# Perceiver block on one core: state sums partly inside the loop, K rotated ahead of the third attention's sum, head groups reordered, clears by ACT, GpSimd's rounding moved

## The reference, cut to what matters

```python
x = x + xattn0(layernorm(x), ctx, ctx)            # 16 heads of 16, 2048 keys
x = x + ssm(layernorm(x), A_log, D, W_xproj)      # 16 states: h = exp(dt*A)*h + dt*B*x; y = C.h + D*x
x = x + lora_moe(layernorm(x))                    # base product + top 2 of 16 rank-16 experts
x = x + xattn1(layernorm(x), ctx, mask)           # one head of 256, 2048 keys, key mask
x = x + attn(layernorm(x))                        # 16 heads of 128: local keys, 8 compressed keys, a sink
x = x + moe(layernorm(x))                         # 8 experts, 256->512->512->256, top 2 by gate
```

## Time and profile before

| | us |
|---|---|
| median of 3 runs (lowest, highest) | 493.5 (490.94, 493.93) |
| the profiled execution | 491.93 |
| its span, first to last instruction | 490.1 |
| TensorE busy | 418.6 (85%) |
| VectorE busy | 334.4 (68%) |
| ACT busy | 267.0 (54%) |
| GpSimd busy | 110.0 (22%) |
| mean granted clock of TensorE | 0.975 |
| share of the chain that ended last: TensorE, VectorE, ACT | 63%, 18%, 7% |

### The profile page before, as it was taken

The page is one execution under the profiler, slowest core; times in us unless marked ns, Lnnn a source line. Parts: engine busy times, 40 slices in busy tenths (PEclk is TensorE's granted clock), DMA queues, the critical chain, the costliest instruction groups (busy, mean ns, idle before and its releaser), DMA issues.

```text
span 490.1 us, 9082 instructions
## 1 busy us (share of the span) xinstructions
PE 418.6 (85%) x3628; PEld 307.4 (63%) x3628; DVE 334.4 (68%) x537; ACT 267.0 (54%) x594; POOL 110.0 (22%) x88
## 2 busy tenths in 40 slices
PE   0168789998978898998998889996999799999997
PEld 0115556665645586486444624445889689999996
DVE  3788766678568977894366654865554788877872
ACT  4405887776758717431233315556771286777762
POOL 3002346001294010000022352233000203333300
PEclk9999999999989999999999979998899799999999
DMA  6599186543751078137200000019300595540000
GB/s 226 130 256 277 25 202 174 141 120 90 185 197 48 3 235 305 44 123 297 95 1 1 0 3 0 1 45 361 109 2 0 168 346 175 172 172 1 1 2 23
DMA packets 25002, 58.28 MB, mean 119 GB/s; under 512 B 5209, under 2 KB 13689, under 8 KB 21114
## 3 DMA queue, kind: packets, MB, share of 16 engines
q1 hardware_dynamic: 24960, 57.69, 37.2%
HBM read 44.77 MB, written 0.29 MB: 92 GB/s over the span
## 4 chain that ended last, share of the span: by engine, by line
PE 63%; DVE 18%; ACT 7%; issue 6%; POOL 2%; DMA 2%; SPq 0%; ACTq 0%; DVEq 0%; POOLq 0%
PE ps L1289 19%; PE ps L1093 9%; PE ps L924 7%; PE ps L911 5%; PE ps L880 4%; DVE mx L1666 3%; ACT reg_b L683 3%; PE ps L959 2%; PE ps L1254 2%; PE ps L1244 2%; PE ps L1243 2%; PE ps L1003 2%; POOL qreg L472 2%; PE ps L1090 1%; DMA x<-in_x 1%
## 5 line engine op out<-in xcount | busy, mean ns | idle before, releaser
L1666 DVE TENSOR_REDUCE mx<-ps 128x1 f32<-128x1024 f32 x64 | 77.0, 1221 | 36.5 <-PE ps L880 24.9
L683 ACT ACTIVATE reg_b<-ps 128x512 f32<-128x512 f32 x128 | 74.9, 598 | 26.6 <-PE ps L911 17.2
L911 PE MATMUL ps<-qreg,reg_b 98*128 98x128 bf16 x512 | 47.3, 225 | 5.7 <-ACT reg_b L683 4.2
L1093 PE MATMUL ps<-reg_b,xT 128*128 128x512 f32 x96 | 49.8, 643 | 0.0
L1289 PE MATMUL ps<-part_a 128*128 128x256 f32 x384 | 48.2, 283 | 0.4 <-DVE part_a L1819 0.4
L911 PEld LDWEIGHTS ps<-qreg,reg_b 98*128 98x128 bf16 x512 | 35.2, 100 | 19.8 <-ACT reg_b L683 9.7
L1289 PEld LDWEIGHTS ps<-part_a 128*128 128x128 f32 x384 | 46.9, 192 | 0.6 <-DVE part_a L1819 0.6
L396 POOL TENSOR_TENSOR rstd<-ve,cf 128x1 f32<-128x1 f32 x12 | 6.8, 567 | 174.0 <-DVE ve L1362 174.0
L822 ACT ACTIVATE reg_a<-ps,b 128x256 f32<-128x256 f32 x64 | 30.2, 472 | 24.4 <-PE ps L1289 24.4
L924 PE MATMUL ps<-reg_b 128*32 128x128 f32 x1024 | 43.0, 285 | 0.3 <-ACT reg_b L683 0.3
L880 PE MATMUL ps<-reg_b,qreg 96*128 96x512 bf16 x96 | 34.3, 427 | 10.2 <-DMA reg_b<-reg_b 7.5
(11 more groups left out here) (279 smaller groups left out, 849.1 us busy)
## 6 DMA issues: line engine op xcount, KB each, us to landing
reg_b<-in_w SPq DMA_DIRECT2D x16, 512.0 KB, 7.6
reg_b<-in_w SPq DMA_DIRECT2D x8, 1024.0 KB, 7.3
reg_b<-reg_b SPq DMA_DIRECT2D x56, 128.0 KB, 3.2
reg_b<-in_w_qkv SPq DMA_DIRECT2D x3, 2048.0 KB, 7.5
reg_b<-reg_a SPq DMA_DIRECT2D x40, 128.0 KB, 3.2
reg_a<-in_ctxK SPq DMA_DIRECT2D x4, 1024.0 KB, 7.5
reg_a<-in_ctx SPq DMA_DIRECT2D x8, 512.0 KB, 4.7
reg_b<-bc_mem SPq DMA_DIRECT2D x4, 1024.0 KB, 6.6
```

What stands on the lines that cost most here:

```text
L683: sc.activation(pT[n % 3], score_b[n % 2], ACT.Exp).then_inc(S("exp_done"), 1)
L911: mm = pe.matmul(cols, kS[g % 3][0:SROWS, c // 8, j, P * (c % 8):P * (c % 8 + 1)], qT[b][0:SROWS, HPG * hg + j, :], start=not last, stop=True)
L1093: mm = pe.matmul(bank(b, n % 2), xT[b][:, i, :], w_qkv[j][:, i, 512 * n:512 * (n + 1)], start=False, stop=i == KD - 1)
L1666: ve.reduce_max(mx[:, piece // 2, piece % 2:piece % 2 + 1], score_a[m % 2].rearrange("p i k -> p (i k)"), X_AXIS).then_inc(S("max_done"), 1)
```

## The change

- `sum_states(0, 0)` goes into the last group of the loop, four states each behind chunks 9, 11, 13 and 15; VectorE's products with C and scans take turns for it.
- Behind the loop: 18 fillers first, `x_to_columns(2, 0)` before `step_sizes(1)`, `lora_products(0)` before `state_maps(1)`; ACT and VectorE follow. The key mask is loaded earlier, to another place, and computed earlier; bias0 counts on another semaphore.
- `square(0, 1)` on ACT ahead of `exp3(1)`; `rotated_to_columns(0, 1)` and its copies behind the third attention's output product of batch 1; `add3(1)` and the normalisation behind the whole of `rope_k(0)` instead of within it.
- `clear_values` on ACT, as a copy scaled by zero.
- Head groups: group 0's transposes and mixing ahead and between the scores of groups 1 and 2; VectorE copies the mixed values of group n-2, not n-1.
- GpSimd rounds expert 0's weights only after six groups' weights are normalised (`pr_norm` 12), and those of expert 1 after `x_split`. VectorE's rests of expert 0 all move into the end of the fourth attention. 24 fillers between the last two transposes of x. GpSimd also waits for `nm_done` 6 within the decay exponents.

```diff
 xmask = view(reg_b, 18432, 2048, BF16)
-mask8 = reg_b[0:1, 12544:12544 + NB * KEYS // 4]
+mask8 = reg_b[0:1, 8192:8192 + NB * KEYS // 4]
 mask_row = xmask[0:1, :]
...
     values_in(NG - 1)
+    load(mask8, io["mask"], "mask_in")
...
     sp.wait_ge(S("hc_done"), KD)
-    load(mask8, io["mask"], "mask_in")
-    load(bias0, io["bias0"].partition_broadcast(P), "mask_in")
+    load(bias0, io["bias0"].partition_broadcast(P), "ssm_in")
     load(ctxT[:, 0, :, :], io["ctxT"][0].rearrange("(h p) k -> p h k", p=P), "ctxT_in0")
...
         for n in range(0, NS, 4):
+            if (h, n) == (0, 12):
+                pool.wait_ge(S("nm_done"), 6)
             pool.tensor_tensor(decay[0][:, h, n:n + 4],
...
-    def clear_values(b):
...
-        pool.wait_ge(S("x_done1"), (4, 3)[b])
-        pool.memset(cvs[b][:, :, :, :], 0.0).then_inc(S("cleared"), 1)
...
     compressed_inv_rms(0)
-    clear_values(1)
     rotated_inv_rms(0, 1)
     inv_sqrt(4, 1)
-    clear_values(0)
+    pool.wait_ge(S("xn_done1"), 5)
     compressed_values(0)
...
     pool.wait_ge(S("expert_in0"), 48)
+    pool.wait_ge(S("pr_norm"), 12)
     round_weights(0, 0, "w13_high")
...
     inv_sqrt(5, 1)
-    for b in range(NB):
-        pool.wait_ge(S(f"x_done{b}"), 5)
+    pool.wait_ge(S("x_split"), NB)
     for e in range(1, NE):
...
+    def clear_values(b):
...
+        if b == 0:
+            sc.wait_ge(S("p3T_ps"), 8)
+        sc.wait_ge(S(f"x_done{b}"), 3)
+        sc.activation(cvs[b].rearrange("p g j d -> p (g j) d"), ident.unsqueeze(1).to_broadcast([P, NH, HD]),
+                      ACT.Copy, scale=0.0).then_inc(S("cleared"), 1)
...
     transposed_x(1, 1)
+    transposed_x(2, 0)
     copy_z(1)
     softplus_exp(1)
-    transposed_x(2, 0)
     hidden_exp(0)
...
     transposed_x(3, 1)
+    clear_values(1)
+    square(0, 1)
     rotated_columns(0, 0)
...
     projected(0, 2, range(0, 1))
-    for i in range(2):
+    for i in range(4):
         p3_columns(1, i)
-    square(0, 1)
-    for i in range(2, 4):
-        p3_columns(1, i)
+    clear_values(0)
     projected(0, 2, range(1, 2))
+    rotated_columns(0, 1)
     transposed_x(4, 1)
...
     block_columns(1)
-    rotated_columns(0, 1)
     key_tail(0)
...
-    for n in range(NB * NHG):
+    weight_columns(0)
+    weights(1)
+    for n in range(1, NB * NHG):
         if n + 1 < NB * NHG:
...
-    def sum_states(b, h):
+    def sum_states(b, h, states=range(NS)):
...
         pe.wait_ge(S("hc_done"), KD * b + h + 1)
-        for n in range(NS):
+        for n in states:
             mm = pe.matmul(bank(b, 0)[:, P * h:P * (h + 1)], state[b][:, h, n, :], ident, start=n == 0, stop=n == NS - 1)
-        if h == KD - 1:
+        if h == KD - 1 and n == NS - 1:
             mm.then_inc(S("y_ps"), 1)
...
               (5, 2): [(keep_busy, 6, 18)],
-              (5, 4): [(misc_read, "o_all", 5), (state_maps, 0)],}
+              (5, 4): [(misc_read, "o_all", 5), (state_maps, 0)]}
+    for i in range(4):
+        beside[7, 9 + 2 * i] = [(sum_states, 0, 0, range(4 * i, 4 * i + 4))]
     read_before_rows = {2: ("qT_sb", 4), 3: ("qT_sb", 6), 5: ("z_sb", 1), 6: ("bc_copied", 1)}
...
-    sum_states(0, 0)
     sum_states(0, 1)
+    keep_busy(7, 18)
     x_to_columns(1, 1)
     keep_busy(7, 4)
+    x_to_columns(2, 0)
     step_sizes(1)
+    lora_products(0)
     state_maps(1)
-    keep_busy(7, 3)
-    x_to_columns(2, 0)
-    keep_busy(7, 6)
-    lora_products(0)
     keep_busy(7, 6)
...
     projection(0, 2, range(1, 2))
+    rotated_to_columns(0, 1)
     x_to_columns(4, 1)
...
     block_entries(1)
-    rotated_to_columns(0, 1)
     projection(1, 1, range(2, 4))
...
     rotated_to_columns(1, 1)
-    pe.wait_ge(S("kT_tail"), 4)
-    pe.wait_ge(S("qkT_sb"), 16)
-    pe.wait_ge(S("proj_sb"), len(PROJECTIONS))
-    scores4(1)
     pe.wait_ge(S("cvs_done"), HPG * NB)
...
-    for n in range(NB * NHG):
+    weights_to_columns(0)
+    pe.wait_ge(S("kT_tail"), 4)
+    pe.wait_ge(S("qkT_sb"), 16)
+    pe.wait_ge(S("proj_sb"), len(PROJECTIONS))
+    scores4(1)
+    scores4(2)
+    mix_values(0)
+    for n in range(1, NB * NHG):
         if n + 2 < NB * NHG:
...
         weights_to_columns(n)
-        if n >= 1:
+        if n >= 2:
             mix_values(n - 1)
...
     for b in range(NB):
+        if b == 1:
+            keep_busy(7, 24)
         pe.wait_ge(S(f"x_done{b}"), 5)
...
     def lora_add(b):
-        ve.wait_ge(S("mask_in"), 32)
+        ve.wait_ge(S("ssm_in"), 48)
         link(ve.tensor_tensor(x[b][:, :], x[b][:, :], bias0, ALU.add))
...
-        ve.wait_ge(S("mask_in"), 32)
+        ve.wait_ge(S("mask_in"), 16)
         ve.tensor_scalar(mask_row[0:1, :], mask8.bitcast(U8), 16.0e30, -16.0e30, ALU.mult, ALU.add)\
...
     scan(0, 0)
+    read_states(0, 0)
     scan(0, 1)
-    read_states(0, 0)
     read_states(0, 1)
+    key_mask()
+    add_inputs(0)
     weigh_outputs(1)
...
     ln_stats(1, 1)
-    add_inputs(0)
-    ln_apply(1, 1)
-    key_mask()
     add_states(0)
     ln_stats(2, 0)
+    ln_apply(1, 1)
     ln_apply(2, 0)
...
     max3(1, 1)
-    rope_k(0, [(add3, 1), (ln_stats, 4, 1), (ln_apply, 4, 1)])
+    rope_k(0, [])
+    add3(1)
+    ln_stats(4, 1)
+    ln_apply(4, 1)
     block_scores(1)
...
             score_max(1)
+        if n >= 2:
+            mixed(n - 2)
         if n + 2 < NB * NHG:
             score_max(n + 2)
-        if n >= 1:
-            mixed(n - 1)
     lower_weights(0, 0)
+    lower_weights(0, 1)
+    mixed(NB * NHG - 2)
+    lower_weights(0, 2)
     for b in range(NB):
...
             .then_inc(S("g_shift"), 1)
-    lower_weights(0, 1)
-    lower_weights(0, 2)
     def gate_weights(b):
```

## The result

The changed kernel takes 479.15 us (median of four runs, 478.81 to 483.96), the kernel before 492.42 (four runs, 490.94 to 493.93): a ratio of 0.975, with a 95% interval of 0.971 to 0.979. The forecast was 481.0. The profiled execution took 479.39 us with a span of 477.6, against 490.1 before: 12.5 less. The median fell by 13.3, and the single executions of the changed kernel spread by 5 us.

A forecast was written before the change was run, and what follows sets the result against it. The kernel was taken as bound by hand-offs, with TensorE's gaps each followed by half clock. 0.4 - 7.6 - 6.3 + 1.8 = -11.7 from 491.93 gave 480.2, by medians 481.8; predicted 481.0, range 477 to 486.

The forecast's parts named there:

- part D: Up to the experts, 380 to 397 us: fillers help hidden1, half clock falls on hidden2; +1.8, from -1.7 to +3.3.
- Part A: State sums moved into the first attention's loop, 164 to 186 us: +0.4 us, from -1.5 to +1.5.
- 0.47 of each 0.89 is covered by ACT and 0.42 is not: In the loop, each insertion of four sums takes 0.89 us, of which ACT's time hides 0.47.
- B is just hidden: Behind the loop, the B matrix lands at 191.6, 2 us later, yet in time for state_input at 191.52 + 0.4.
- Part B: K rotated ahead of the third attention's sum, 262 to 304 us: -7.6 us, from -4 to -8.5.
- The 0.4 put down for hand-offs to ACT: Around K's rotation, 0.4 us taken off the sum of gains 1.2 + 3.84 + 3.0.
- Part C: Head groups, 330 to 363 us: smaller gaps, full clock and a shorter period; -6.3 us, from -2.2 to -7.
- the rivals on the period: Head groups: the period stays at 4.48 and only the gaps are won; 483 us, chance 0.13.
- on K being late: Projections: K is late or another gap holds, and half clock is back; 484.8 us, chance 0.10.
- on the slower loop: Head group loop runs at half clock, 7.8 us a group instead of 4.05; 500 us, chance 0.03.
- on no fall of the clock in D: Before the experts, the clock doesn't fall, as gaps are shorter than the earlier 3.03 us; 479.0 us, chance 0.22.
- the one on B's matrix: Behind the first attention's loop, B's matrix lands late, its load sharing queues with the ctxT load; 482.5 us, chance 0.07.

The follow-up runs named there:

- three: Changed kernel with GpSimd waiting for the seventh maxima, fillers between hidden1(0) and hidden2(0), and state_maps(1) ahead of lora_products(0): 475.14 us, ratio 0.966.
- pool_clear: Changed kernel with the two clears back on GpSimd in their old places, K's rotation still ahead of the third attention's sum: 480.48 us, ratio 0.977.
- casts_early: Changed kernel without GpSimd's wait for six groups' weights, so its three casts of expert 0 start early: 482.93 us, ratio 0.980.
- K late: Changed kernel with K's square, reduction, rotation and transposes back in their old places, clears still on ACT: 485.27 us, ratio 0.986.

## Why the prediction was right, and where its steps were off

The forecast of 481.0 was 1.9 above the median, and each part came within about 1 us in the table. That their errors partly cancel in the sum (-0.8) is luck, and so in part is part D. One slip made no difference: the range took A's bounds as 1.1 either way, while -1.5 lies 1.9 from +0.4.

**Part A, +0.4 forecast, +1.0 measured, and 0.35 brought along.** The order of events was right: states ready in time, y early (1.0 us instead of 1.9), the maps late, LoRA's step behind their copy. The failed step is "0.47 of each 0.89 is covered by ACT and 0.42 is not": an insertion costs 0.57. Four sums take about 1.0 within the loop, where the prediction took the 0.89 of those behind it; the cover of 0.47 was right. So the sums behind the loop start 2.4 later counted from the scan, not 1.7. With y 1.0 early and nothing waiting for it, the whole part is a loss; the runs with it undone show this twice. The prediction's own sign of being wrong, LoRA's first step later than by 1 us, was even met in the timeline (186.21 against 185.03, 1.18 later); counted from the first scan it is 0.83. "B is just hidden" held too, and `three` found its edge: 1.2 us earlier and it isn't.

**Part B, -7.6 forecast, -8.35 measured.** Each step came within 1.2 us: exp3(1) 1.5 earlier (1.53), K's reduction at 266.85 (265.65), rotation ready 276.9 (276.0), x normalised 280.0 (279.1), no gap, full clock. About 0.9 of each delay is what had come in ahead of this part, 1.35 instead of 0.4. I gave TensorE 1.2 of exp3's 1.53; `pool_clear` shows it keeps 1.5. The 0.4 put down for hand-offs to ACT didn't come, by subtraction; no run isolates it.

**Part C, -6.3 forecast, -7.3 measured** (from the first exponential to attention_out, 39.12 to 31.79), a little beyond its bound of -7. The gaps were right (-2.3). The period was right in its cause, wrong in two sizes that nearly cancel: 3.77, not 4.05, as ACT sets it (it shows no idle there, while TensorE manages 3.66 in `casts_early`, 344.68 to 348.34) without the 0.17 of hand-offs that I added to TensorE's 3.88, but over three periods, not four or five: 2.1 against 1.8. The rest, 5.2 against 4.5, fell in the first three groups; their gaps are 2.3 of it, and how the other 2.9 divide between full clock and order no run shows. The casts' place, which I costed only through the gaps, carries 2.2 of this.

**Part D, +1.8 forecast, +1.8 measured.** Hidden1(0) began 1.0 earlier (0.85) and took 3.15, not half of 5.13, which is hidden. The gate's shifts stretched to 0.82 and 0.69 and put ACT's second exponential 1.1 later behind hidden1's start, where I had 1.4. Hidden2 had its fall (+2.15 on the 39 matmuls; forecast +2.0). The mechanism is confirmed from both sides, without the 24 fillers and with more of them behind hidden1. The exact hit is luck: the seven other kernels that share these fillers have 13.56 to 14.76 in the last interval, which would make part D +0.3 to +1.5.

The bulk of the gain is thus B and C; the rivals on the period, on K being late, on the slower loop and on no fall of the clock in D didn't happen; the one on B's matrix didn't in the changed kernel, but does 1.2 us from it. Of the signs named, the period came at 3.77 for 4.05 and the last loop pairs at 2.11 for 1.96; the others were seen as told. Of -11.7 and the measured -12.5, the errors were +0.9 in A with what it brought along, -0.75 in B, -1.0 in C.

What stays open: where a single execution's 1 to 5 us come from. Part is the first attention's start, whose third maxima were at 71.79 in the changed kernel and at 74.30 with K late, before any edit acts; the profile shows waits there that differ, not why. Part is the clock, next.

## What to carry to other kernels

Fillers belong where TensorE is about to become the bound, not ahead of work whose end is hidden: a fall of the clock cost nothing under hidden1 and 1.0 to 2.5 us under hidden2. Count GpSimd's instructions against VectorE's short chains: a one-microsecond GpSimd step turned a chain of four 0.2 us steps into 3.7, and one well-aimed wait took that away, though one step of the next chain was then held. And work moved into a loop "beside" another engine was only free up to TensorE's own slack in that loop (0.47 a pair here); the rest was paid at the loop's end, where the longest chain begins. Last, look at how an interval spreads over kernels that share it before giving its difference to an edit: here one repeated to 0.05 us and another only to 1.5.

## What the runs showed of the hardware

The same gaps don't always bring the same clock. Ahead of batch 0's fourth transposes TensorE waits 1.11 us and then 0.55, to 0.02 us alike in all profiles without fillers there. In the profile with part A undone the clock then fell; in that of the changed kernel it didn't (stretches table, columns as above; first the changed kernel):

```profile
226.00:228.00 2.00, 2.00 (x18) 1.74 (x17) 0.89 (x3) 0.31 (x1) 0.00 (x0) 1.00 1.01 430
228.00:230.00 2.00, 2.00 (x21) 2.00 (x19) 0.00 (x0) 0.00 (x0) 0.00 (x0) 1.00 0.14 57
```
```profile
226.00:228.00 2.00, 2.00 (x13) 1.84 (x11) 0.89 (x3) 0.31 (x1) 0.00 (x0) 0.63 1.00 426
228.00:230.00 2.00, 2.00 (x11) 2.00 (x11) 0.00 (x0) 0.00 (x0) 0.00 (x0) 0.51 0.02 8
```

32 state sums took 5.47 us instead of 3.84, and the end was 1.65 later. The clock fell so in three of the thirteen profiles without fillers there, and behind the gap of 1.92 us in one of two. A single profile can thus blame or clear an edit wrongly. And which VectorE step a GpSimd cast holds went by the operation, not by its size. On the same 128x8 tile, RECIPROCAL took its usual 0.19 to 0.20 beside a cast in two kernels, while the scale behind it took 0.49 and 0.85 instead of 0.17, and the step with two inputs 1.23.
